# Two softmax attentions: the per-head mask moves from the keys to the queries

## The reference

```python
def _L0_attn_ref(x, mask, Wq, Wk, Wv, Wout):
    B, S, D, H = (4, 256, 128, 16)
    DH = D // H
    n, s, d = x.shape
    scale = 1.0 / np.sqrt(DH).astype(np.float32)
    q = (x @ Wq).reshape(n, s, H, DH)
    k = (x @ Wk).reshape(n, s, H, DH)
    v = (x @ Wv).reshape(n, s, H, DH)
    attn = jnp.einsum('nqhd,nkhd->nqkh', q, k) * scale
    attn = jax.nn.softmax(attn, axis=-2)
    z = jnp.einsum('nqkh,nkhd->nqhd', attn, v).reshape(n, s, d)
    z = jnp.einsum('nqd,de->nqe', z, Wout)
    return x + z
...
x = x + _L0_attn_ref(_layernorm(x, axis=-1), L0_attn_mask, L0_attn_Wq, L0_attn_Wk, L0_attn_Wv, L0_attn_Wout)
x = x + _L0_xattn_ref(_layernorm(x, axis=-1), ctx_1024, ctx_1024, L0_xattn_w_out, L0_xattn_b_out)
```

## Time and profile before

| | us |
|---|---|
| median of 3 runs | 600.41 (596.93 to 601.2) |
| the profiled execution, its own time | 599.32 |
| span of that execution (first to last instruction) | 597.2 |
| TensorE matmuls busy (modelled ends) | 469.0, 79% of the span |
| DVE busy | 332.1, 56% |
| ACT busy | 240.4, 40% |
| POOL busy | 209.2, 35% |
| granted TensorE clock, mean | 0.88 of full |

### The profile page before, as it was taken

How to read it: one execution, slowest core, us unless ns; L and a number is a source line. 1 busy time by engine, 2 the same in 40 slices (tenths; PEclk the granted TensorE clock), 3 DMA queues, 4 the chain that set the end, 5 groups by cost and what they waited for, 6 DMA issues and landing times. The chain is left out here.

```text
span 597.2 us, 13480 instructions
## 1 busy us (share of the span) xinstructions
PE 469.0 (79%) x5103; PEld 374.5 (63%) x5103; DVE 332.1 (56%) x917; ACT 240.4 (40%) x514; POOL 209.2 (35%) x234
## 2 busy tenths in 40 slices
PE   3899999999986978999999988992663332499950
PEld 1587777777763757899988877781553221266630
DVE  5567677777753535666666652637755667011114
ACT  3766666666552326555555522230220000132313
POOL 3556687799133214000000010316430000557750
PEclk9899999999996999999999987997575555599995
DMA  7970312200000002000000003000024000333317
GB/s 234 386 292 6 143 61 61 63 3 2 4 1 1 0 7 76 1 0 0 0 0 0 0 2 88 19 1 0 1 77 134 1 0 0 103 96 106 113 33 211
DMA packets 31461, 34.72 MB, mean 58 GB/s; under 512 B 5562, under 2 KB 25079, under 8 KB 31289
## 3 DMA queue, kind: packets, MB, share of 16 engines
q1 hardware_dynamic: 29208, 29.50, 15.6%
q0 software_dynamic: 2064, 4.60, 2.4%
q10 hardware_dynamic: 144, 0.00, 0.0%
HBM read 28.65 MB, written 5.46 MB: 57 GB/s over the span
## 5 line engine op out<-in xcount | busy, mean ns | idle before, releaser
L473 DVE TENSOR_REDUCE at_nmax<-bank 128x4 bf16<-128x512 f32 x128 | 82.5, 686 | 44.0 <-PE bank L569 44.0
L413 ACT ACTIVATE at_p<-bank 128x512 f32<-128x512 f32 x128 | 69.2, 596 | 38.2 <-PE bank L588 38.2
L95 POOL TENSOR_TENSOR var<-var,eps 128x12 f32<-128x12 f32 (+1 forms) x8 | 1.6, 206 | 176.4 <-DVE var L88 176.4
L1902 POOL DMA_INDIRECT mo_rows<-mo_n_rows,mo_src_row x24 | 23.0, 959 | 71.3 <-POOLq L1610 64.3
L582 PE MATMUL bank<-ident_b,at_nmax 128*128 128x128 bf16 x512 | 42.8, 221 | 4.3 <-DVE at_nmax L473 3.4
L582 PEld LDWEIGHTS bank<-ident_b,at_nmax 128*128 128x128 bf16 x512 | 30.7, 98 | 18.9 <-issue 9.3
L1975 ACT ACTIVATE mo_h<-bank,mo_b 128x308 f32<-128x308 f32 x32 | 16.5, 517 | 47.5 <-PE bank L1938 47.5
L608 PE MATMUL bank<-at_p,at_v 128*32 128x128 f32 x1024 | 34.7, 276 | 0.9 <-DVE x L490 0.9
L1946 PE MATMUL bank<-mo_w,mo_h 128*128 128x128 f32 (+1 forms) x192 | 33.0, 294 | 1.3 <-ACT mo_h L1975 1.3
L1946 PEld LDWEIGHTS bank<-mo_w,mo_h 128*128 128x128 f32 (+1 forms) x192 | 24.3, 173 | 12.1 <-ACT mo_h L1975 5.3
L1081 PE MATMUL bank<-li_v,li_am 128*128 128x65 f32 x256 | 30.4, 272 | 0.5 <-issue 0.5
(11 more groups left out here) (280 smaller groups left out, 1193.1 us busy)
## 6 DMA issues: line engine op xcount, KB each, us to landing
fo_w<-in_up_stages SPq DMA_DIRECT2D x9, 512.0 KB, 9.3
fo_w<-in_down_stages SPq DMA_DIRECT2D x9, 512.0 KB, 4.7
at_k_ctx<-in_ctx_heads SPq DMA_DIRECT2D x1, 4096.0 KB, 23.9
mo_w<-in_L_ffn_W SPq DMA_DIRECT2D x16, 256.0 KB, 3.1
mo_planes<-ro_zeros POOLq DMA_DIRECT2D x1, 2048.0 KB, 9.1
mo_got<-mo_planes SPq DMA_DIRECT2D x8, 256.0 KB, 5.1
x<-in_x SPq DMA_DIRECT2D x4, 256.0 KB, 3.6
au_ctx<-in_ctx SPq DMA_DIRECT2D x4, 256.0 KB, 3.4
```

The costliest lines, as they stand in the source:

```text
L413: act.activation(m.p[:, s % 2, J * g:J * g + J, :], bank_t[g][:, :].rearrange("p (j t) -> p j t", j=J), ACT.Exp, scale=scale).then_inc(exp ...
L473: dve.tensor_reduce(m.nmax[:, J * g:J * g + J], bank_s[g % 2][:, :].rearrange("p (j t) -> p j t", j=J), AX.X, ALU.max, negate=True).then_i ...
L1902: pool.indirect_dma_start(out=rows[0:m, e % 2, r, :], out_offset=None, in_=n_rows, in_offset=bass.IndirectOffsetOnAxis(ap=src_row[0:m, til ...
```

## The change

The queries are masked instead of the keys. `m.q` grows by a factor J: ACT's copy of a q round out of PSUM becomes four copies, each with a per-partition scale, column j of the 0/1 mask; the first waits for the mask's load. Keys stay as they are: `k_j`, its three slots, POOL's `mask_keys` and the semaphore `k_made` go, and the context keys are loaded once, 1 MB. In `scores` a pair of row groups now takes eight bf16 matmuls (for each j, for both groups) with one head's masked queries stationary and 128 key columns moving, each writing 128 columns of its bank. In `shifted_scores` each row group takes one fp32 matmul with 128 unmasked key columns stationary and 512 masked query columns moving.

```diff
--- before.py
+++ after.py
@@ -113,10 +113,9 @@
 
         self.n = sb("at_n", [T, 2, Q, D])
         self.nT = sb("at_nT", [D, Q * T])
-        self.q = sb("at_q", [D, 2, Q, T])
+        self.q = sb("at_q", [D, 2, Q, J, T])
         self.kT = sb("at_kT", [D, 2, Q, T])
-        self.k_j = sb("at_k_j", [D, K_SLOTS, J, T])
-        self.k_ctx = sb("at_k_ctx", [D, B, J, T])
+        self.k_ctx = sb("at_k_ctx", [D, B, T])
         self.v = sb("at_v", [T, 2, Q, G * J, 32])
         self.nmax = sb("at_nmax", [T, G * J], BF16)
         self.p = sb("at_p", [T, 2, G * J, T])
@@ -133,7 +132,6 @@
 
 
 Q = 4
-K_SLOTS = 3
 GROUPS = B // Q
 V = 2 * B
 LO, HI = 5, 4
@@ -205,10 +203,10 @@
         return slice(32 * g, 32 * g + 32)
 
     def queries(s, g):
-        return m.q[rows(g), s // Q % 2, s % Q, :]
+        return m.q[rows(g), s // Q % 2, s % Q, :, :]
 
     def keys(s, g):
-        return m.k_j[rows(g), s % K_SLOTS, :, :] if s < B else m.k_ctx[rows(g), s - B, :, :]
+        return m.kT[rows(g), s // Q % 2, s % Q, :] if s < B else m.k_ctx[rows(g), s - B, :]
 
     with nc.Block() as block:
         @block.sync
@@ -234,7 +232,7 @@
             sp.dma_start(m.w_out[1][:, :], a["L0_xattn_w_outT"]).then_inc(out_in, 16)
             sp.dma_start(m.bias[:, :], a["L0_xattn_b_out"].partition_broadcast(T)).then_inc(ctx_in, 16)
             sp.dma_start(m.ctx[:, :, :], a["ctx_1024"].rearrange("b t d -> t b d")).then_inc(ctx_in, 16)
-            sp.dma_start(m.k_ctx[:, :, :, :].rearrange("p b j t -> p (b j t)"), a["ctx_heads"]).then_inc(k_ctx_in, 16)
+            sp.dma_start(m.k_ctx[:, :, :].rearrange("p b t -> p (b t)"), a["ctx_rows"]).then_inc(k_ctx_in, 16)
             sp.dma_start(f.down_w[:, :], a["W_conT"]).then_inc(down_in, 16)
             sp.dma_start(f.up_bias[:, :], a["up_bias_col"]).then_inc(small_in, 16)
             for i, src in enumerate(("L0_ffn_b_con", "L0_ffn_down_bias")):
@@ -274,14 +272,6 @@
                 pool.tensor_tensor(m.shift[:, seqs], m.neg_mean[:, seqs], core.rstd[:, seqs, 0], ALU.mult)\
                     .then_inc(rstd, 1)
 
-            def mask_keys(s):
-                g = s // Q
-                pool.wait_ge(copied, done_after["k", g])
-                if s >= K_SLOTS:
-                    pool.wait_ge(shifted, G * (s - K_SLOTS + 1))
-                pool.tensor_tensor(m.k_j[:, s % K_SLOTS, :, :], over(m.kT[:, g % 2, s % Q, :], J),
-                                   m.mask[:, :].unsqueeze(2).to_broadcast([D, J, T]), ALU.mult).then_inc(k_made, 1)
-
             def residual(g):
                 seqs = slice(Q * (g % GROUPS), Q * (g % GROUPS) + Q)
                 pool.wait_ge(normed, Q * (g + 1))
@@ -336,17 +326,11 @@
             inverse(0)
             inverse(1)
             residual(0)
-            pool.wait_ge(mask_in, 16)
-            mask_keys(0)
             inverse(2)
-            mask_keys(1)
             residual(1)
-            mask_keys(2)
             inverse(3)
             step = 0
             for i in range(V):
-                if i + K_SLOTS < B:
-                    mask_keys(i + K_SLOTS)
                 if var_at(i - 1) is not None:
                     inverse(var_at(i - 1))
                 if i in (3, 7):
@@ -399,12 +383,16 @@
                     act.activation(value_slots(m.v[:, g % 2, :, :, :]),
                                    bank[:, :].rearrange("p (a k d) -> p a k d", k=2, d=DH), ACT.Copy)\
                         .then_inc(copied, 1)
+                elif kind == "k":
+                    act.activation(m.kT[:, g % 2, :, :], bank[:, :].rearrange("p (b t) -> p b t", b=Q), ACT.Copy)\
+                        .then_inc(copied, 1)
                 else:
-                    if kind == "k" and g >= 2:
-                        act.wait_ge(k_made, Q * (g - 1))
-                    dst = m.kT if kind == "k" else m.q
-                    act.activation(dst[:, g % 2, :, :], bank[:, :].rearrange("p (b t) -> p b t", b=Q), ACT.Copy)\
-                        .then_inc(copied, 1)
+                    if g == 0:
+                        act.wait_ge(mask_in, 16)
+                    for j in range(J):
+                        ins = act.activation(m.q[:, g % 2, :, j, :], bank[:, :].rearrange("p (b t) -> p b t", b=Q),
+                                             ACT.Copy, scale=m.mask[:, j:j + 1])
+                    ins.then_inc(copied, 1)
 
             def exps(s, g):
                 act.wait_ge(shifted, G * s + g + 1)
@@ -560,15 +548,17 @@
                 if pair == 0:
                     pe.wait_ge(copied, done_after["q", s // Q])
                     if s < B:
-                        pe.wait_ge(k_made, s + 1)
+                        pe.wait_ge(copied, done_after["k", s // Q])
                     elif s == B:
                         pe.wait_ge(k_ctx_in, 16)
                 if s or pair:
                     pe.wait_ge(maxed, G * s + 2 * pair)
-                for g in (2 * pair, 2 * pair + 1):
-                    pe.matmul(bank_s[g % 2][:, :], bf16_head(queries(s, g)),
-                              bf16_head(keys(s, g).rearrange("p j t -> p (j t)")), start=True, stop=True)\
-                        .then_inc(scored, 1)
+                for j in range(J):
+                    for g in (2 * pair, 2 * pair + 1):
+                        mm = pe.matmul(bank_s[g % 2][:, j * T:(j + 1) * T], bf16_head(queries(s, g)[:, j, :]),
+                                       bf16_head(keys(s, g)), start=True, stop=True)
+                        if j == J - 1:
+                            mm.then_inc(scored, 1)
 
             def maxima(s, groups):
                 if s >= V:
@@ -583,12 +573,9 @@
                                   core.ident_b[:, :], start=(j == 0), stop=False, skip_group_check=True)
 
             def shifted_scores(s):
-                for j in range(J):
-                    for g in range(G):
-                        mm = pe.matmul(bank_t[g][:, j * T:(j + 1) * T], keys(s, g)[:, j, :], queries(s, g),
-                                       start=False, stop=(j == J - 1), skip_group_check=True)
-                        if j == J - 1:
-                            mm.then_inc(shifted, 1)
+                for g in range(G):
+                    pe.matmul(bank_t[g][:, :], keys(s, g), queries(s, g).rearrange("p j t -> p (j t)"),
+                              start=False, stop=True, skip_group_check=True).then_inc(shifted, 1)
 
             def values(i):
                 if i >= 2:
@@ -2104,11 +2091,7 @@
     from concourse.bass_utils import run_bass_kernel_spmd as _run
 
     arrays = {k: np.ascontiguousarray(v) for k, v in inputs.items() if k != "L0_attn_mask"}
-    heads = np.zeros((G, J, DH, B, J, T), np.float32)
-    ctxT = inputs["ctx_1024"].transpose(2, 0, 1).reshape(G, J, DH, B, T)
-    for j in range(J):
-        heads[:, j, :, :, j, :] = ctxT[:, j]
-    arrays["ctx_heads"] = heads.reshape(D, B * J * T)
+    arrays["ctx_rows"] = np.ascontiguousarray(inputs["ctx_1024"].transpose(2, 0, 1).reshape(D, B * T))
     arrays["L0_xattn_w_outT"] = np.ascontiguousarray(inputs["L0_xattn_w_out"].T)
     for name, w, forward in (("up_stages", "L0_ffn_up_weights", True), ("down_stages", "L0_ffn_down_weights", False)):
         arrays[name] = _butterfly_stages(inputs[w], forward)
```

More of the change, by code:

```diff
@@ L166, in attention @@
      down_in, bias_in, small_in, made, zeroed, stat, varied, rstd, next_var, next_rstd, decay_ready, raised, normed, x_res,
-     k_made, v_made, filled, copied, scored, maxed, shifted, exped, pv_done, mix_copied, mixed, rden_done, o_done,
+     v_made, filled, copied, scored, maxed, shifted, exped, pv_done, mix_copied, mixed, rden_done, o_done,
      x_done, folded, bias_folded, bias_out, bias_back) = core.sems(
@@ L171, in attention @@
         "down_in bias_in small_in made zeroed stat varied rstd next_var next_rstd decay_ready raised normed x_res "
-        "k_made v_made filled copied scored maxed shifted exped pv_done mix_copied mixed rden_done o_done "
+        "v_made filled copied scored maxed shifted exped pv_done mix_copied mixed rden_done o_done "
         "x_done folded bias_folded bias_out bias_back")
```

## The result

The changed kernel takes 604.29 us, median of 10 executions (602.6 to 607.52), the kernel before 600.34 in executions beside them: ratio 1.0073, 95% interval 1.0042 to 1.0103. So it is slower by 0.7%, by 3.95 us, where the forecast was +3.8 and 603.1. The profiled executions stand 4.5 us apart, 603.86 against 599.32 (spans 601.7 and 597.2).

The account below looks back on a forecast made before the run. A chain through TensorE was taken to set the pace of 32 visits. ACT's copies +4.4 us and TensorE -0.6 gave +3.8 on the profiled 599.32: 603.1 us, own range 599 to 607, with rivals 598 to 615.

Parts of the forecast that it names:

- ACT's bursts: Four query copies per round on ACT, 0.58 us apart, make the next exponentials 1.03 late; ACT's sum +4.4 us.
- The start: Group 0's query copies delay every ACT link behind them, up to the first exponential at 24.58: +0.62 us.
- TensorE a visit: First and second scores together on TensorE: -0.02 us a visit, -0.6 us over 32 visits.
- -0.04 for L588: Second scores: two 512-column passes per row group take 0.86 us instead of 0.90 for eight narrow ones.
- +0.02 for L569: First scores: eight 128-column matmuls per pair take about as long as two of 512; 0.01 more per pair.
- POOL, the context load, the mask's wait: nothing: POOL's 16 dropped maskings, the context load's cut to 1024 KB and the mask wait's move to ACT change no time.
- 1 fell: Rival: weight loads set the second scores' step, so they take 0.48 instead of 0.90 us; 591 us in all, chance 0.07.
- 2 fell: Rival: weight loads exposed in the first scores, 0.48 instead of 0.24 us a pair; 618 us, half exposed 611; chance 0.15.
- 3 fell: Rival: the second scores' four row tiles run in order, 2.15 instead of 0.90 us; 644 us, chance 0.07.
- 4 fell: Rival: ACT's bursts are mostly absorbed, 600 to 601 us; counted within the forecast's own range.

Follow-up runs that it names:

- no_burst: The changed kernel with only the first of four scaled query copies per round, the other heads' queries left zero: 601.33 us, 1.0010 of the kernel before.
- burst_alone: The kernel before plus three more scaled copies of each query round on ACT into a spare tile nobody reads: 606.23 us, ratio 1.0083.
- warm_less: The changed kernel plus 4 and 4 idle fp32 128-column matmuls on TensorE in the waits at the start: 605.16 us, 1.0075 of the kernel before.
- small_tiles: The changed kernel with the second scores as 16 matmuls of 128 columns again: 606.37 us, 1.0088 of the kernel before.
- norm_later: The changed kernel with ACT's normalise behind a query copy moved to the visit after it: 602.0 us, 1.0036 of the kernel before.
- g_major: The changed kernel with a pair's eight first-score matmuls issued group by group instead of alternating: 606.91 us, 1.0086 of the kernel before.
- later_warm: The changed kernel with the normalise a visit later and 4 and 4 idle matmuls at the start: 602.77 us, 1.0042 of the kernel before.

## Why the prediction held, and where it didn't

1. **ACT's bursts, right.** Copies were forecast 0.58 apart; four take 2.42 us, which with 0.69 for one is a pitch of 0.58. The lateness was to be 1.03, is 1.02; what the next visit absorbs was to be 0.37 and 0.49, is 0.35 and 0.48. Groups 2 to 7 sum to 3.11 us against 3.10 forecast. no_burst and burst_alone show that the slowing stands and falls with these copies.
2. **The start, mis-sized.** The step said that every link behind on ACT hangs on the one before, +0.62; it measured +1.22. On ACT alone the step is right: the value copy and the normalises come 0.57 later. But the copy of the transposes behind them (L377 at 20.97) waits for TensorE, and the forecast left TensorE's clock out (named only among what isn't seen). In these two executions it fell about 2 us sooner and stayed at half for longer, which stretched transposes and second scores: 0.57 queue, 0.46 transposes, the last 0.19 behind the second scores. warm_less, with the clock at full, gives 0.71 back.
3. **TensorE a visit, wrong in sign.** -0.04 for L588 and +0.02 for L569 were to give -0.02; measured +0.03 to +0.04. The row tiles gain 0.03 (small_tiles). The term that failed is the cover: the forecast took the loads of the narrow first scores as hidden, which they are, but not that the first weight load of the second scores had been hidden beneath their 512 columns and now lies open by 0.05 in groups 0 and 1. The length of the first pass shows the open load. From the start of the last maxima to the first matmul of the values pass 1.53 us before (143.23 to 144.76), 1.56 after (144.04 to 145.60) and 1.60 in small_tiles (145.60 to 147.20), so nearly all of the drift lies in this stretch; that the load behind the narrow first scores causes it is argued from these lengths, since the one attempt to cover it made things worse. In before the line at the end of the stretch reads

```profile
144.76 0.32 PE L608 MATMUL bank<-at_p,at_v 128*32 128x128 f32 x4
```

4. **POOL, the context load, the mask's wait: nothing, right.** no_burst keeps these changes too, and from group 2 on its visits are 0.03 to 0.04 longer than before's, none shorter but the last (4.51 against 4.54).
5. **Behind the stage: not foreseen.** The stage ends 6.07 us later (the last addition to x at 187.04 against 180.97), the kernel 4.5. Most of the difference lies at one place, near the end of the linear attention, and it is TensorE's clock again. In before the clock is at half while the stage's last transposes and projection run; in after the same work, some 6 us later, still runs at full, and the clock falls only behind it (0.50 in 363.6:370.3). Windows and the last projection, in before and in after:

```profile
355.10:365.30 10.20, 7.81 (x25) 6.08 (x26) 4.03 (x17) 1.53 (x4) 1.21 (x2) 0.50 0.11 22
...
357.01 2.07 PE L1095 MATMUL bank<-li_wo,li_yT 128*128 128x128 f32 x8 [0.78 <-DVE li_yT L943]
```

```profile
361.00:363.50 2.50, 1.53 (x11) 1.29 (x12) 0.82 (x2) 0.00 (x0) 0.00 (x0) 1.00 0.00 0
...
362.63 1.29 PE L1082 MATMUL bank<-li_wo,li_yT 128*128 128x128 f32 x8 [0.78 <-DVE li_yT L930]
```

   The addition of x near the end of that stage (359.12 before, 363.96 after) is only 4.84 late. Other executions show other offsets there (norm_later goes from +2.58 to +1.70 and later to +1.86), so this isn't a property of the change. It made the sum agree better than its terms do: ahead of the stage's end the terms were 2.3 us too low in these two executions (start, group 1's stalls, TensorE, end of the stage), and 1.5 came back behind it. The size of the bursts was forecast; that the whole agrees to 0.2 us in the median is in part luck.
6. **Rivals.** 1 fell: a visit didn't get shorter by 0.33, and the two 512-column passes of fp32 in a row group start 0.48 (groups 0 and 1) and 0.53 (2 and 3) apart, not 0.24. 2 fell, but for the 0.05 of point 3: first scores take 0.40 a pair. 3 fell: side by side. 4 fell: no more was absorbed than the forecast had it.

## What to carry to other kernels

An engine that is idle for a third of a stage (ACT was busy 98.7 of 151.0 us) can still set the cost of a change. Extra work on it costs its whole lateness where it comes in a burst ahead of something that another engine waits for: price the burst at its place in the engine's queue, then subtract what the next period absorbs. Then look at what else stands in that queue: moving one short normalise out of the burst's shadow gave back 2.3 us by the visits' periods, more than half of what the change had cost, with the copies unchanged. And when a wide instruction becomes several narrow ones of the same length, ask what was hidden beneath it.

## What the runs showed of the chip beyond that

- Full-array matmuls (the maxima, on all 128 rows) between two sets of row-tiled ones (32 rows each) end their overlap here: the second scores follow row-tiled first scores at 0.06 us or start beside them, but follow the maxima at 0.15 (147.09 behind the last of four that start 0.056 apart from 146.76), with every load open. That made 0.17 us a visit.
- Idle matmuls kept the granted clock at 1.00 in waits of 1.5 and 1.7 us, in the second of which it fell to half without them (warm_less against after). Their count must fit the wait: 7 and 9 delayed the transposes by 1.08 us.
- There are stalls without a cause in the profile, in TensorE's own queue, mostly within visits 3 and 4 (the first is 0), where the DMA engines still are busy (a share of 0.39 in both windows below). The table of waits of TensorE in g_major from 34 to 40 us and in burst_alone from 40 to 52 us (us in total, times, longest):

```profile
PE bank L595 <- issue: 2.5, 1, 2.5
```

```profile
PE bank L615 <- issue: 4.3, 1, 4.3
```

  They lie in visit 3 in g_major and, with 1.6 us, in later_warm, in visit 4 in burst_alone, and lengthen that visit by 2 to 6 us; in g_major and burst_alone the clock fell in the same stretch (0.77 and 0.86 in these windows). They are probably part of why single executions of one kernel lie up to 9 us apart, which wasn't tried. What the queue waited for stays open. From the ninth visit on only small_tiles shows such waits (0.4 and 0.2 us); the comparisons rest on periods that recur from group to group.
